# A new beginning for a per-image mixed 3x3 convolution block: image 0 in halves, weights convolution by convolution, a ring of four buffers

## The chip, the cores and the metric

The kernel runs on one core of one Trainium2 chip. The metric is the device time of one execution in microseconds; the number compared is the median of several runs. One further execution is recorded by the profiler.

## What is computed

Sixteen images of 32 channels and 96 x 96 pixels in float32. Each is normalised channel by channel, and for each image a softmax gate over seven experts mixes its own two sets of 3x3 kernels:

```python
x_n     = (x - mean) / sqrt(var + 1e-5)                 # per image and channel
gate    = softmax(mean(x_n) @ gate_w.T + gate_b)         # 7 values per image
kw1,kb1 = sum_e gate[e] * experts_1[e] + conv1           # kernels and bias of this image
kw2,kb2 = sum_e gate[e] * experts_2[e] + conv2
out     = x + x_n + conv3x3(relu(conv3x3(x_n, kw1) + kb1), kw2) + kb2
```

## The kernel before

Channels and row groups share the 128 partitions (32 channels x 4 rows), so an image is a tile `img` of 128 x 24 x 96, in a ring of six. Both convolutions work on float16 pairs: a value is a high part (HI) and a low part (LO), and three products (HI x HI, HI x LO of the weights, LO x HI) are added in PSUM. A convolution is five groups (`pg0` to `pg4`) of 18 matmuls: per product and kernel column one with the straight weights and tile (`a`) and one with the crossed ones (`c`), whose partition halves are exchanged. The two of a pair run side by side in the array.

The steps of an image are these. `load` (SP queue). `statistics` and `aggregate` (VectorE), `gather_rows` (TensorE, `pstat`), `channel_moments` (VectorE), `coefficients` (GpSimd), which give mean and scale and the gate's input `gwp`. `logits` (TensorE), `softmax_in`, `exponentials` (ScalarE), `softmax_out`. `mixture`, seven VectorE steps over `bank` (all kernels of both convolutions, 386 wide) into `mix`; `weights_high` casts the high part on ScalarE, `weights` subtracts the low part on VectorE. The crossed copy comes by DMA (`cross_weights`), for the first two images (EARLY) by two VectorE copies (`cross_early`). The input: `normalise` writes float32 `xh` and `high_part` the HI half of `a1` on ScalarE, `low_part` the LO half on GpSimd in four pieces, `cross1` sends both to `c1` by DMA. Then conv1; `hidden` (ScalarE, twice per group: `hid` float32 and HI of `a2`), `hidden_low` (VectorE), `clear_rim`, `cross2` (two ScalarE copies), conv2; `residual` (GpSimd), `finish` (VectorE), `store`.

Each engine has its list of instructions written out by hand: a beginning, and then `slot(s)` once per image. In slot s TensorE does conv1 of image s and conv2 of image s-1, with `gather_rows` of image s+2 between groups 3 and 4 of conv1. TensorE's beginning ends with four of the five conv1 groups of image 1 and slot 1 opens with `gather_rows` of image 3, then group 4 of image 1. Lists are in order: an instruction waits for semaphores, and all behind it on its engine waits too.

The raw kernels (`natural`) arrive on ScalarE's DMA queue, are spread (`pad_kernels`), turned by TensorE (`transpose_kernels(n)`, n = 0 to 3 for conv1, 4 to 7 for conv2) and copied into `bank` by ScalarE (even n) and VectorE (odd n).

## Time and profile before

| | |
|---|---|
| median of 3 runs | 365.44 us (365.11 to 365.81) |
| profiled execution, device time | 366.37 us |
| its span, first to last instruction | 364.6 us |
| busy: TensorE matmul / VectorE / ScalarE / GpSimd | 87% / 79% / 69% / 53% |
| chain that ended last: TensorE / VectorE / DMA | 60% / 19% / 10% |
| mean granted TensorE clock | 0.98 |

The device time is 1.8 us longer than the span in the profiled execution. A share of busy time is a mean over a beginning, a long regular stretch and an end; the stretches differ, and so they are read apart.

### The profile page before, as it was taken

How to read it: one execution, taken by the hardware profiler on the slowest of the kernel's cores; microseconds unless marked ns; L12 is line 12 of the kernel's file. 1: busy time of each engine (PE TensorE's matmuls, PEld its weight loads, DVE VectorE, ACT ScalarE, POOL GpSimd, SP SyncE). 2: the span in 40 equal slices, each digit the busy share in tenths (PEclk: the TensorE clock that was granted, in tenths of full speed). 3: DMA queues.
4: the chain of work that ended last, by engine and by line, in shares of the span. 5: the costliest groups of instructions: out<-in, count | busy, mean ns of one | idle time of the engine just before them, and what ended most of it. 6: DMA issues, size and time to landing. Idle time of an engine off the chain costs nothing.

```text
span 364.6 us, 7708 instructions
## 1 busy us (share of the span) xinstructions
PE 317.4 (87%) x2983; PEld 200.6 (55%) x2983; DVE 288.0 (79%) x651; ACT 252.8 (69%) x278; POOL 192.9 (53%) x236
## 2 busy tenths in 40 slices
PE   2327664499999999999899989999999999999994
PEld 2216432257565656565566646575756565676552
DVE  4699945698989989898979896989989898693432
ACT  1155219896878778787869695878887797965710
POOL 8039517492838475665739391848475656921000
PEclk9999989599999999999999999999999999999999
DMA  9932930599989797989997899979898977575055
GB/s 197 222 70 57 227 77 3 120 167 202 210 186 211 177 216 179 211 174 205 191 217 145 201 199 220 173 180 219 186 211 188 211 173 151 122 174 142 0 131 130
DMA packets 109379, 60.86 MB, mean 167 GB/s; under 512 B 102944, under 2 KB 105248, under 8 KB 109344
## 3 DMA queue, kind: packets, MB, share of 16 engines
q1 hardware_dynamic: 108544, 59.79, 78.9%
q10 hardware_dynamic: 608, 0.59, 0.6%
q8 instruction: 23, 0.38, 0.5%
q14 instruction: 12, 0.10, 0.1%
q0 software_dynamic: 192, 0.01, 0.0%
HBM read 19.47 MB, written 18.87 MB: 105 GB/s over the span
## 4 chain that ended last, share of the span: by engine, by line
PE 60%; DVE 19%; DMA 10%; SPq 3%; ACT 3%; POOL 2%; issue 2%; ACTq 0%; DVEq 0%; POOLq 0%
PE pg L376 56%; DVE mix L646 9%; DMA wts<-wts 7%; DVE a L677 3%; DVE wts L663 3%; DMA c<-a 2%; PE pg L339 2%; DVE stats L601 2%; PE pstat L359 2%; POOL a L865 1%; SPq L260 1%; DMA natural<-in_L_conv_conv_w 1%; SPq L296 1%; SPq L287 1%; ACT xh L491 1%
## 5 line engine op out<-in xcount | busy, mean ns | idle before, releaser
L376 PE MATMUL pg<-a,wts 128*64 128x480 f16 (+1 forms) x1440 | 292.2, 362 | 11.3 <-DMA c<-a 6.3
L376 PE MATMUL pg<-c,wts 128*64 128x480 f16 (+1 forms) x1440 | 297.7, 366 | 0.0
L376 PEld LDWEIGHTS pg<-c,wts 128*64 128x64 f16 x1440 | 154.5, 110 | 72.2 <-issue 1.1
L376 PEld LDWEIGHTS pg<-a,wts 128*64 128x64 f16 x1440 | 154.8, 110 | 43.3 <-issue 8.7
L865 POOL TENSOR_TENSOR a<-xh,a 128x576 f16<-128x576 f32 x64 | 79.1, 1268 | 13.4 <-POOL col L873 9.3
L534 ACT ACTIVATE hid<-pg,col 128x480 f32<-128x480 f32 x80 | 52.5, 657 | 46.7 <-PE pg L376 37.1
L646 DVE SCALAR_TENSOR_TENSOR mix<-bank,gate,mix 128x386 f32<-128x386 f32 x96 | 73.9, 770 | 2.4
L846 POOL TENSOR_TENSOR col<-col,minus_half 128x1 f32<-128x1 f32 x16 | 13.5, 841 | 111.6 <-DVE col L619 111.6
L550 ACT COPY c<-a 64x2352 f32<-64x2352 f32 x32 | 68.9, 2152 | 2.1 <-DVE a L677 1.9
L677 DVE TENSOR_TENSOR a<-hid,a 128x480 f16<-128x480 f32 x80 | 52.5, 657 | 21.2 <-ACT a L534 20.9
L693 DVE SCALAR_TENSOR_TENSOR img<-pg,img 128x480 f32<-128x480 f32 (+1 forms) x80 | 48.2, 632 | 13.6 <-PE pg L376 13.1
L879 POOL TENSOR_SCALAR img<-img,col 128x1152 f32<-128x1152 f32 x32 | 57.9, 1817 | 0.1
L534 ACT ACTIVATE a<-pg,col 128x480 f16<-128x480 f32 x80 | 52.5, 656 | 0.0
L601 DVE BATCH_NORM_STATS2 stats<-img 128x6 f32<-128x384 f32 x96 | 45.6, 544 | 0.1
L491 ACT ACTIVATE xh<-img,col 128x2304 f32<-128x2304 f32 x16 | 36.9, 2306 | 11.3 <-POOL col L847 11.3
L496 ACT ACTIVATE a<-img,col 128x2304 f16<-128x2304 f32 (+1 forms) x17 | 37.3, 2194 | 6.5 <-POOL col L847 6.5
L663 DVE TENSOR_TENSOR wts<-mix,wts 128x384 f16<-128x384 f32 x16 | 20.6, 1288 | 0.3 <-ACT wts L519 0.3
L359 PE MATMUL pstat<-triples,same 128*128 128x12 f32 x32 | 7.0, 293 | 15.4 <-DVE triples L608 15.4
L519 ACT CAST wts<-mix 128x384 f16<-128x384 f32 x16 | 8.2, 512 | 15.9 <-DVE mix L646 15.9
L359 PEld LDWEIGHTS pstat<-triples,same 128*128 128x128 f32 x32 | 5.5, 215 | 21.4 <-DVE triples L608 16.0
L616 DVE COPY col<-pstat 128x1 f32<-128x1 f32 x16 | 2.5, 157 | 18.6 <-PE pstat L359 18.6
L339 PE MATMUL pg<-ident,padded 128*128 128x128 f32 x24 | 5.6, 424 | 8.4 <-DVE padded L707 8.4
(61 smaller groups left out, 143.4 us busy)
## 6 DMA issues: line engine op xcount, KB each, us to landing
c<-a SPq DMA_DIRECT2D x28, 588.0 KB, 7.0
img<-in_x SPq DMA_DIRECT2D x56, 288.0 KB, 7.0
out<-img SPq DMA_DIRECT2D x60, 180.0 KB, 3.0
out<-img SPq DMA_DIRECT2D x60, 108.0 KB, 2.6
wts<-wts SPq DMA_DIRECT2D x28, 96.0 KB, 2.5
c<-a SPq DMA_DIRECT2D x8, 294.0 KB, 5.9
img<-in_x SPq DMA_DIRECT2D x16, 144.0 KB, 5.0
out<-img SPq DMA_DIRECT2D x4, 120.0 KB, 2.1
```

The costliest lines, as they stand in the source:

```text
L376: last = nc.tensor.matmul(pg[g][side * 64:side * 64 + 64, at:at + nb * W].rearrange("p (b w) -> p b w", w=W), wts[s.c % WSETS][kind][:, v, ...
L491: nc.scalar.activation(xh[t.parity][:, :, :], img[t.ring][:, :, :], ACT.Identity, bias=c[:, NBIAS:NBIAS + 1], scale=c[:, RSTD:RSTD + 1]).t ...
L496: return nc.scalar.activation(a1[t.parity][:, HI, b0:b1, 1:1 + W], img[t.ring][:, b0:b1, :], ACT.Identity, bias=c[:, NBIAS:NBIAS + 1], sca ...
L534: last = nc.scalar.activation(o, pg[g][:, 0:SPG * W].rearrange("p (b w) -> p b w", w=W), ACT.Relu, bias=c[:, B1:B1 + 1], scale=HS / WS)
L550: last = nc.scalar.copy(d, a[:, :, first:first + NB * RP // 2])
L601: last = nc.vector.bn_stats(stats[t.ring][:, j, :], flat[:, j * SC:(j + 1) * SC])
L646: nc.vector.scalar_tensor_tensor(out=mix[:, (e + 1) % 2, :, :], in0=bank[:, e, :, :], scalar=gate[t.ring][:, e:e + 1], in1=bank[:, E, :, : ...
L663: nc.vector.tensor_tensor(st[:, :, LO, :], mix[:, E % 2, :, 0:TAPS], st[:, :, HI, :], ALU.subtract).then_inc(w_ok, 1)
L677: nc.vector.tensor_tensor(a2[s.parity][:, LO, j0:j1, 1:1 + W], hid[g_parity(s, g)][:, :, :], a2[s.parity][:, HI, j0:j1, 1:1 + W], ALU.subt ...
L693: nc.vector.scalar_tensor_tensor(out=r, in0=pg[g][:, 0:(b1 - b0) * W].rearrange("p (b w) -> p b w", w=W), scalar=1.0 / (WS * HS), in1=r, o ...
L865: last = nc.gpsimd.tensor_tensor(a1[t.parity][:, LO, b0:b1, 1:1 + W], xh[t.parity][:, b0:b1, :], a1[t.parity][:, HI, b0:b1, 1:1 + W], ALU. ...
L879: last = nc.gpsimd.tensor_scalar(img[t.ring][:, b0:b1, :], img[t.ring][:, b0:b1, :], c[:, RS1:RS1 + 1], c[:, RB:RB + 1], ALU.mult, ALU.add)
```

## The change

SP: only image 0 is loaded in halves (`x_half`); image 1 comes whole. The high and low parts of images 0 and 1 are crossed in halves of the rows, HI of image 0 ahead of the load of image 2, LO behind it. ScalarE: the six loads of `natural` wait for the first half of image 0. Images 0 and 1 get their weights for one convolution at a time: `mixture_early` runs seven steps 193 wide, `weights_early` subtracts and copies for one convolution; conv1's come first and release `w_early`, conv2's come later and release `w_crossed`. `low_part` of an early image waits for `w_early`. TensorE runs conv1 of images 0 and 1 in two passes, all groups with HI, then all with LO, and all five groups of image 1 are done ahead of slot 1; transposes 6 and 7 stand within image 0's conv1. `hid` becomes a ring of four, two of them in `natural`, which is free by then, and `hidden` waits for the `hidden_low` of four groups earlier instead of two. The slots keep their order, and slot 0 of ScalarE and GpSimd is written out in the beginning.

```diff
+        spare = natural[:, :, :, :].rearrange("p a b c -> p (a b c)")
+        hid = [h[:, :, :] for h in hid] + [spare[:, i * SPG * W:(i + 1) * SPG * W].rearrange("p (j w) -> p j w", w=W)
+                                           for i in range(2)]
...
             load(Sample(0, 0))
             load(Sample(0, 1))
+            cross1_early(Sample(0, 0), HI, 0)
+            cross1_early(Sample(0, 0), HI, 1)
             load(Sample(0, 2))
-            cross1(Sample(0, 0))
+            cross1_early(Sample(0, 0), LO, 0)
+            cross1_early(Sample(0, 0), LO, 1)
+            cross1_early(Sample(0, 1), HI, 0)
+            cross1_early(Sample(0, 1), HI, 1)
             load(Sample(0, 3))
-            cross1(Sample(0, 1))
+            cross1_early(Sample(0, 1), LO, 0)
+            cross1_early(Sample(0, 1), LO, 1)
...
+            early_conv1(first, 0, HI)
+            early_conv1(first, 1, HI)
+            transpose_kernels(6)
+            transpose_kernels(7)
+            early_conv1(first, 2, HI)
+            gather_rows(second)
...
+            gather_rows(third)
+            for g in range(GRP):
+                early_conv1(second, g, HI)
+            early_conv1(second, 0, LO)
+            early_conv1(second, 1, LO)
+            logits(third)
...
-                run(conv1_group, s, 0, 1, 4)
+                run(conv1_group, s, 0, 2, 4)
...
             def load_kernels():
+                act.wait_ge(x_half, LOAD)
...
-                if not (s.known(0) and g < 2):
-                    act.wait_ge(lo2_ok, s.number * GRP + g - 1)
+                if s.number * GRP + g >= len(hid):
+                    act.wait_ge(lo2_ok, s.number * GRP + g + 1 - len(hid))
...
+            def mixture_early(t, v, e0, e1):
...
+                for e in range(e0, e1):
+                    if e > 0:
+                        dve.wait_ge(mix_step, (weight_sets(t, v) - 1) * (E - 1) + e)
+                    nc.vector.scalar_tensor_tensor(
+                        out=mix[:, (e + 1) % 2, v, :], in0=bank[:, e, v, :], scalar=gate[t.ring][:, e:e + 1],
+                        in1=bank[:, E, v, :] if e == 0 else mix[:, e % 2, v, :],
+                        op0=ALU.mult, op1=ALU.add).then_inc(mix_step if e < E - 1 else mix_ok, 1)
...
+            def weights_early(t, v):
+
+                dve.wait_ge(whi_ok, weight_sets(t, v))
+                st, cr = wts[t.c % WSETS][STRAIGHT], wts[t.c % WSETS][CROSSED]
+                link(nc.vector.tensor_tensor(st[:, v, LO, :], mix[:, E % 2, v, 0:TAPS], st[:, v, HI, :], ALU.subtract))
+                for a, b in ((0, 1), (1, 0)):
+                    last = nc.vector.tensor_copy(halves(cr)[a][:, v].rearrange("p a b -> p (a b)"),
+                                                 halves(st)[b][:, v].rearrange("p a b -> p (a b)"))
+                if v == 0:
+                    last.then_inc(w_early, 1)
+                else:
+                    last.then_inc(w_crossed[t.ring], 32)
...
             coefficients(Sample(0, 0))
+            low_part(Sample(0, 0))
             coefficients(Sample(0, 1))
-            low_part(Sample(0, 0), 0, PARTS)
-            low_part(Sample(0, 1), 0, PARTS)
+            low_part(Sample(0, 1))
+            coefficients(Sample(0, 2))
+            residual_bias(Sample(0, 0))
+            residual(Sample(0, 0))
```

Three places show how the lists move. On VectorE the first is its start, after the constants; before, it read (a row is line, operation, output and inputs with their numbers):

```order
L707 COPY padded<-natural 128x3x96 x2
L735 TENSOR_SCALAR bank<-pg1 128x4x96
L735 TENSOR_SCALAR bank<-pg3 128x4x96
L707 COPY padded<-natural 128x3x96 x2
L735 TENSOR_SCALAR bank<-pg1 128x4x96
L735 TENSOR_SCALAR bank<-pg3 128x4x96
L601 BN_STATS stats0<-img0 128x6 x6
L606 BN_AGGR mv0<-stats0 128x2
```

The same place of VectorE's list now:

```order
L677 BN_STATS stats0<-img0 128x6 x6
L692 BN_AGGR mv0<-stats0 128x2
L693 TENSOR_SCALAR triples0<-row,mv0 128x4
L694 TENSOR_SCALAR triples0<-row,mv0 128x4
L820 COPY padded<-natural 128x3x96 x2
L702 COPY col0<-pstat 128x1
L703 BN_AGGR col0<-pstat 128x2
L704 TENSOR_SCALAR col0<-col0 128x1
L705 TENSOR_SCALAR col0<-col0 128x1
```

The statistics of image 0 have moved ahead of the kernels, and the moments of image 0 stand behind the first spreading of the kernels.

The second place is VectorE ahead of the statistics of image 3. Before:

```order
L677 TENSOR_TENSOR a2_0<-hid0,a2_0 128x5x96
L684 MEMSET a2_0 32x2x96
L601 BN_STATS stats3<-img3 128x6 x6
L625 SCALAR_TENSOR_TENSOR logit2<-pgate,gbias 128x7
L628 TENSOR_REDUCE col2<-logit2 128x1
L677 TENSOR_TENSOR a2_1<-hid1,a2_1 128x5x96
L606 BN_AGGR mv3<-stats3 128x2
```

Now, from the end of image 0's `hidden_low` steps:

```order
L743 SCALAR_TENSOR_TENSOR mix<-bank,gate0,mix 128x193 x6
L770 TENSOR_SCALAR col0<-mix 128x1
L711 SCALAR_TENSOR_TENSOR logit2<-pgate,gbias 128x7
L714 TENSOR_REDUCE col2<-logit2 128x1
L755 TENSOR_TENSOR wts0_0<-mix,wts0_0 128x192
L757 COPY wts0_1<-wts0_0 64x384 x2
L743 SCALAR_TENSOR_TENSOR mix<-bank,gate1 128x193
L743 SCALAR_TENSOR_TENSOR mix<-bank,gate1,mix 128x193 x6
L770 TENSOR_SCALAR col1<-mix 128x1
L755 TENSOR_TENSOR wts1_0<-mix,wts1_0 128x192
L757 COPY wts1_1<-wts1_0 64x384 x2
L677 BN_STATS stats3<-img3 128x6 x6
```

The conv2 weights of images 0 and 1 now stand between the last `hidden_low` of image 0 and the statistics of image 3.

The third place is ScalarE behind group 4 of image 0's `hidden`. Before:

```order
L534 ACTIVATE a2_0<-pg4,col0 128x5x96
L496 ACTIVATE a1_0<-img2,col2 128x24x96
L550 COPY c2_0<-a2_0 64x2352 x2
L510 ACTIVATE expo2,col2<-logit2,col2 128x7
L534 ACTIVATE hid1<-pg0,col1 128x480
```

And now:

```order
L600 ACTIVATE a2_0<-pg4,col0 128x5x96
L577 CAST wts0_0<-mix 128x192
L616 COPY c2_0<-a2_0 64x2352 x2
L541 ACTIVATE xh0<-img2,col2 128x2304
L554 ACTIVATE a1_0<-img2,col2 128x24x96
L577 CAST wts1_0<-mix 128x192
L571 ACTIVATE expo2,col2<-logit2,col2 128x7
L600 ACTIVATE hid1<-pg0,col1 128x480
```

The two casts of conv2 weights stand ahead of and behind `cross2` of image 0 and the input of image 2.

## Rows read from the trace of the kernel before

**Rows 1.** Chain of waits, regular stretch: start us, us, what ran.

```profile
98.28 3.09 DMA wts<-wts
101.41 7.53 PE pg L376 x71
...
214.68 4.65 DMA wts<-wts
```

**Rows 2.** Busy time by stretch: PE, PEld, DVE, ACT, POOL, then clock, DMA, GB/s.

```profile
60.00:69.00 9.00, 0.58 (x4) 0.55 (x6) 5.06 (x16) 8.96 (x11) 4.83 (x4) 0.66 0.16 31
...
90.00:108.95 18.95, 18.70 (x183) 11.52 (x181) 17.24 (x39) 15.27 (x17) 11.75 (x13) 1.00 0.97 199
```

**Rows 3.** Timeline, TensorE: start us, us, line, operation, count, [idle before <-releaser].

```profile
6.94 2.79 PE L339 MATMUL pg<-ident,padded 128*128 128x128 f32 x12 [6.94 <-DVE padded L707]
...
33.15 0.35 PE L376 MATMUL pg<-a,wts 128*64 128x384 f16 x1 [0.60 <-DVE wts L670]
...
48.99 0.32 PE L376 MATMUL pg<-a,wts 128*64 128x384 f16 x1 [5.13 <-DMA c<-a]
...
68.42 0.60 PE L359 MATMUL pstat<-triples,same 128*128 128x12 f32 x2 [9.51 <-DVE triples L608]
...
82.13 0.36 PE L376 MATMUL pg<-c,wts 128*64 128x480 f16 x1
```

**Rows 4.** Start: timeline of two rows, and DMA issues with us to landing.

```profile
1.68 0.48 ACTq L474 DMA_DIRECT2D natural<-in_L_conv_conv_w  x1
...
5.88 0.92 DVE L707 COPY padded<-natural 128x288 f32<-128x288 f32 x2 [2.42 <-DMA natural<-in_L_conv_conv_w]
...
natural<-in_L_conv_conv_w ACTq DMA_DIRECT2D x1, 36.0 KB, 4.1
...
img<-in_x SPq DMA_DIRECT2D x2, 144.0 KB, 3.7
```

**Rows 5.** Timeline of VectorE and GpSimd, 14 to 74 us.

```profile
14.63 2.86 DVE L601 BATCH_NORM_STATS2 stats<-img 128x6 f32<-128x384 f32 x6
...
22.56 0.17 DVE L625 SCALAR_TENSOR_TENSOR logit<-pgate,gbias 128x7 f32<-128x7 f32 x1
...
23.64 0.23 DVE L636 TENSOR_SCALAR gate<-expo,col 128x7 f32<-128x7 f32 x1
...
25.54 3.24 DVE L646 SCALAR_TENSOR_TENSOR mix<-bank,gate,mix 128x386 f32<-128x386 f32 x5
...
28.80 5.40 POOL L865 TENSOR_TENSOR a<-xh,a 128x576 f16<-128x576 f32 x4
...
30.49 2.60 DVE L670 COPY wts<-wts 64x768 f16<-64x768 f16 x2
...
34.92 7.45 DVE L646 SCALAR_TENSOR_TENSOR mix<-bank,gate,mix 128x386 f32<-128x386 f32 x6
...
43.54 0.72 DVE L670 COPY wts<-wts 64x768 f16<-64x768 f16 x2
...
70.88 0.88 POOL L846 TENSOR_TENSOR col<-col,minus_half 128x1 f32<-128x1 f32 x1 [4.58 <-DVE col L619]
...
73.34 0.47 POOL L856 TENSOR_TENSOR gwp<-table,col 128x7 f32<-128x7 f32 x1
```

**Rows 6.** Timeline of ScalarE and VectorE, 42 to 77 us, and one DMA issue.

```profile
42.82 0.65 ACT L534 ACTIVATE hid<-pg,col 128x480 f32<-128x480 f32 x1
...
43.92 0.66 ACT L534 ACTIVATE hid<-pg,col 128x480 f32<-128x480 f32 x1
...
59.02 2.32 ACT L496 ACTIVATE a<-img,col 128x2304 f16<-128x2304 f32 x1
61.23 4.31 ACT L550 COPY c<-a 64x2352 f32<-64x2352 f32 x2
...
76.52 1.45 DVE L663 TENSOR_TENSOR wts<-mix,wts 128x384 f16<-128x384 f32 x1
...
wts<-wts SPq DMA_DIRECT2D x2, 96.0 KB, 2.2
```

More of the change, by code:

```diff
@@ L49 @@
 EARLY = 2
-WARM = 7
+WARM = 8
 PARTS = 4
@@ L371, in products @@
                 for image, weight in pairs:
-                    if early(s) and v == 0 and g == 0 and image == LO:
-                        wait_low_part(s)
                     for kw in range(3):
@@ L744, in _ @@
             row_constants()
+            statistics_first(0)
+            statistics_first(1)
+            aggregate(first)
             pad_kernels(0)
+            channel_moments(first)
+            repeat_table()
             copy_kernels(1)
+            copy_table()
             copy_kernels(3)
             pad_kernels(1)
+            softmax_in(first)
+            softmax_out(first)
+            mixture_early(first, 0, 0, E)
+            weights_early(first, 0)
             copy_kernels(5)
+            statistics(second)
@@ new lines, in _ @@
+            weights_early(second, 0)
+            channel_moments(third)
+            hidden_low(first, 0)
+            clear_rim(first, 0)
+            hidden_low(first, 1)
+            hidden_low(first, 2)
+            hidden_low(first, 3)
+            hidden_low(first, 4)
+            clear_rim(first, GRP - 1)
+            mixture_early(first, 1, 0, E)
+            softmax_in(third)
+            weights_early(first, 1)
+            mixture_early(second, 1, 0, E)
+            weights_early(second, 1)
```

339 lines of the change are left out of this document (190 added, 149 removed).

## Prediction, written before the changed kernel was run

> **What bounds the kernel now.** I read the chain of waits first, then the busy time by stretch, then the timelines of the beginning. In the regular stretch the chain of one image runs from `gather_rows` through moments, mixture and weights on VectorE to the DMA that crosses the weights, which lands after 3.09 us, and then through four conv1 groups of 7.53 us [rows 1] to the next `gather_rows`. TensorE is busy 18.70 of 18.95 us there [rows 2], so the loop and TensorE are about equally long. Nothing in the slots changes, so what the change is worth is how much sooner the regular stretch is entered. I measure it where conv1 of image 2 begins, at 82.13 us [rows 3].
>
> The beginning before is no TensorE stage. The first conv1 matmul starts at 33.15, behind the crossed weights of image 0; TensorE then waits 5.13 us up to 48.99 for crossed rows, and 9.51 us up to 68.42 for the statistics of image 3 [rows 3]. In that last wait ScalarE is busy 8.96 of 9 us [rows 2]: VectorE cannot finish image 3's `aggregate` before ScalarE has delivered `hidden` of image 1. So a gain at 33 reaches 68 only if it also gets through the lists of ScalarE and VectorE. I follow four stages, each ending at an event all later work needs. All times are my sums unless a row is named.
>
> **Stage A, up to the first conv1 weights.** The kernels' DMAs now wait for half of image 0. Its fourth transfer is issued at about 2.2; transfers of this size issued first landed in 3.7 us [rows 4]. With no kernels beside it I take 6.0 (ends 5.6 and 7.8). Three issues of about 0.48 follow; the last began at 1.68 in the kernel before and landed after 4.1 us, VectorE starting on it at 5.88 [rows 4]. So the kernels are there at 6.0 + 1.0 + 4.1 = 11.1, say 11.2. The statistics of image 0 (2.86 [rows 5]) lie in the wait. Spreading costs 0.92 [rows 4], 12.1; transposing 2.8 [rows 3], 15.0; turning and copying the table 0.8, 15.8. VectorE then copies and spreads for 1.5 more, 17.3, over which `gwp` and `logits` are hidden. Softmax took 1.3 from 22.56 to the end of the gate [rows 5]: 18.6. Seven mixture steps 193 wide: the trace has none. Of 386 one takes 3.24 / 5 = 0.65; a step of 7 elements takes 0.17 to 0.2 [rows 5]. Bounds are half (0.32) and the whole (0.65); fixed part 0.2 plus half of 0.45 gives 0.43, which I take. 7 x 0.43 = 3.0, 21.6. The cast 0.4 (bounded by a `hidden` step, 1.10 / 2 = 0.55 [rows 6]), the subtraction 0.4, two copies at most the 0.72 of double width [rows 5], 0.5: **22.9**. Before it was 33.15, so 10.2 sooner. GpSimd waits for `w_early`, so nothing slows these copies. The crossed HI halves leave at 16.4 and 19.6 and are hidden. Eight warming matmuls end at about 22.3.
>
> **Stage B, up to image 1's conv1 weights.** VectorE: copy 0.6, statistics of image 1 2.9, aggregate 0.7, 27.1. TensorE: twelve pairs (0.2 each), six transposes, six pairs, `gather_rows`, 28.6. Moments 0.5, 29.1. GpSimd from the first coefficient to `gwp` takes 2.9 (70.88 to 73.81 [rows 5]), 32.0; TensorE reaches `logits` of image 1 at 32.3, after 24 pairs: 32.9. VectorE's statistics of image 2 end at 33.2, its load having moved behind image 0's HI crossing; softmax and exponentials, 34.1 on ScalarE. There `hidden` 0 and 1 (1.1 each [rows 6]) and two halves of `normalise` (1.2 each) stand ahead of the cast: 38.7, and VectorE's mixture, done at 37.7, hides behind them. Cast, subtraction and copies: **40.0**. TensorE has waited some 4.5 us by then. Around the wait of 9.51 the granted clock is 0.66 [rows 2, 3]; whether the clock falls here is open, the price is 1.7 us, and it lies on TensorE, which is not late here.
>
> **Stage C, up to the end of image 0's conv2 mixture.** Moments 0.5; five `hidden_low` and two rims 3.3: 43.8. Then seven steps of 0.43, the first two still beside image 1's `low_part` (5.40 for its four pieces, so to 45.4); beside it six full steps took 7.45, or 1.24 each [rows 5]. I take 4.1: **47.9**.
>
> **Stage D, up to `gather_rows` of image 3.** This is the place that gives back most of the gain. ScalarE: cast 0.4, `cross2` 4.3 (4.31), `normalise` 2.2 and `high_part` 2.2 (59.02 to 61.23) [rows 6], and only then the cast of image 1's conv2 weights: 57.4. VectorE has finished their mixture at about 55 and waits for that cast, and the statistics of image 3 are queued behind it. The three steps of `weights_early` then run beside `low_part` of image 2, which starts on the same ScalarE step. Copies of double width took 1.30 each beside such pieces and 0.36 without [rows 5]; ends for the three steps are 0.9 and 3.9, and I take 3.5, since a copy beside GpSimd lasted as long as one of its pieces (5.40 / 4 = 1.35), whatever its own work. 60.9. Statistics 2.9, `hidden_low` 0.6, aggregate 0.7: **65.1**, against 68.42. TensorE has waited since about 51.5.
>
> The Trainium skill (SBUF — State Buffer, SBUF: two separate sides) says that VectorE steps with two SBUF inputs or in a two-port mode and a GpSimd step hold a shared port pair exclusively, the later one blocking for the whole instruction. By it, halving the width buys nothing beside GpSimd, so it speaks against this split; the 1.30 beside 1.35 agrees. With widths scaled instead (0.65 a copy) the sum would be 1.5 us lower.
>
> **Stage E.** From aggregate to the end of `weights` took 68.4 to 77.97 (76.52 + 1.45 [rows 6]), 9.6, in an order that stays: 74.7. Two issues 0.6 and a landing of 2.2 [rows 6]: conv1 of image 2 starts at **77.5**. TensorE's other work in between (conv2 of image 0, nine us and 1.7 for the low clock) ends at about 76, since group 4 of image 1 is gone from there. Before: 82.13. Difference **4.6 us**.
>
> **The ring of four** is costed at nothing: ScalarE's waits for VectorE stand in the beginning alone, and C and D go through other waits. Without it ScalarE's `hidden` 2 to 4 would follow VectorE's steps, a bit over 1 us at C. The profiled execution lies 0.9 above the median (366.37 and 365.44). 366.4 - 4.6 = 361.8 for a profiled one; **360.8** for the median.
>
> **Rivals.**
> (1) The whole 10.2 us is carried through: 355.2. It needs VectorE and ScalarE to be early at stage D; against it stand the 9.1 us of ScalarE work between the two casts. 7%.
> (2) The kernels queue behind image 1's load instead of sharing with it. The load is 1.18 MB, at 0.2 MB per us [rows 2] nearly 6 us; they would be there at about 14: 363.6. Against it: beside image 0's load they landed in 4.1. The Trainium skill (DMA: Bandwidth & Descriptors, Queues, rings and completion order) says that each DMA engine takes turns between its queues by packets, which agrees with that 4.1 and would keep 360.8. 12%.
> (3) Full-width price for half-width steps (0.65): 1.5 at A, 1.5 at C, together 363.8. 10%.
> (4) Slower than before: the weights' DMA in the regular stretch meets other traffic. It is in the chain of seven images; it landed after 3.09 in one and 4.65 in another [rows 1]. The loads and stores follow the new phase. If all seven slip by 1.5, 10.5 is added: 371.3. It decides from 4.6 / 7 = 0.66 us an image. For it: the spread exists; against: every slot restarts from the same `gather_rows`, so the phases repeat. 7%.
> (5) Stage D takes up everything (nothing gained, 365.4): `gather_rows` of image 3 would have to come at 69.7, most of (2) and (3) at once. 5%.
>
> **How the numbers follow.** The forecast case with its own spread holds 59%. The terms' bounds: kernels at 10.1 or 12.7 (with a late half image), steps of 0.32 (1.5 less over A and C), weights at D 0.9 (2.6 less) or 3.9. That is 356 to 363; not all fall together, so 357.3 below, and 364.2 above to take in (2) and (3). A measurement can tell about 0.2% (0.7 us) from no change. Faster than 364.7: (1), (2), nearly all of (3) and the forecast, 0.87; within: 0.05; slower: 0.08.
>
> **What would show it.** First conv1 matmul at about 23; `w_early` of image 1 at 40; a TensorE wait of 10 to 14 us ahead of `gather_rows` of image 3, released by VectorE's `triples`; copies of `weights_early` over 1 us beside GpSimd; a short wait on the crossed weights ahead of conv1 of image 2; intervals between later `gather_rows` as before, near 19.3. The forecast is wrong if image 3's `gather_rows` falls outside 62 to 67, or if the regular stretch changes its period.

## The result: 0.6% slower

Measured again beside each other, the kernel before took 367.56 us (median of 20, 365.11 to 370.25) and the changed one 369.38 (median of 20, 367.18 to 373.1): a ratio of 1.006, 95% interval 1.0037 to 1.0082 (by the two medians alone it is 1.005). The forecast was 360.8 with a range from 357.3 to 364.2, so it was wrong, and on the wrong side. The profiled execution of the changed kernel took 369.45 us; its span was 367.6, against 364.6.

First the chain of waits of the changed kernel (start us, us, what), in the beginning and around the first interval of the regular stretch.

```profile
2.18 3.09 DMA img<-in_x
...
6.21 7.79 DMA natural<-in_L_conv_conv_w
...
14.02 0.90 DVE padded L820 x2
...
79.55 0.52 SPq L320
...
80.11 2.18 DMA wts<-wts
...
89.87 0.34 PE pstat L392 x2
...
97.95 1.04 SPq L320
...
99.04 3.79 DMA wts<-wts
...
102.88 7.53 PE pg L407 x71
110.41 0.32 PE pstat L392 x2
```

Then the timeline of TensorE (start, us, line, tiles, [idle before <-releaser]), to be held against [rows 3].

```profile
25.45 0.35 PE L407 MATMUL pg<-a,wts 128*64 128x384 f16 x1 [1.34 <-DVE wts L757]
...
41.84 0.53 PE L407 MATMUL pg<-a,wts 128*64 128x384 f16 x1 [4.53 <-DVE wts L757]
...
69.97 0.60 PE L392 MATMUL pstat<-triples,same 128*128 128x12 f32 x2 [15.71 <-DVE triples L694]
```

The first conv1 matmul starts at 25.45 instead of 33.15, 7.7 us sooner. Then TensorE waits 15.71 us instead of 9.51, and `gather_rows` of image 3 comes at 69.97, 1.55 later than before (68.42). Conv1 of image 2, my mark for the entry, begins at 82.33 against 82.13. So all of the early gain is gone at the entry. From there to the end some 2.8 us more are lost. I read the slots by the aggregate step that opens `channel_moments` on VectorE, in these two kernels about half a microsecond behind each `gather_rows`: from image 4's to the last one's, eleven intervals, it takes 213.4 us before (90.07 to 303.47) and 216.2 after (90.30 to 306.54). The first of them is 19.31 before and 20.54 after.

Where the time between 42 and 69 went is in VectorE's timeline of the changed kernel.

```profile
42.26 1.36 DVE L790 TENSOR_TENSOR a<-hid,a 128x480 f16<-128x480 f32 x1
...
43.97 1.27 DVE L790 TENSOR_TENSOR a<-hid,a 128x480 f16<-128x480 f32 x1
45.16 3.32 DVE L790 TENSOR_TENSOR a<-natural,a 128x480 f16<-128x480 f32 x2
48.39 0.65 DVE L790 TENSOR_TENSOR a<-hid,a 128x480 f16<-128x480 f32 x1
...
49.85 2.70 DVE L743 SCALAR_TENSOR_TENSOR mix<-bank,gate,mix 128x193 f32<-128x193 f32 x6
...
61.95 1.31 DVE L755 TENSOR_TENSOR wts<-mix,wts 128x192 f16<-128x192 f32 x1 [2.94 <-ACT wts L577]
63.30 2.40 DVE L757 COPY wts<-wts 64x384 f16<-64x384 f16 x2
65.73 2.86 DVE L677 BATCH_NORM_STATS2 stats<-img 128x6 f32<-128x384 f32 x6
```

And GpSimd beside it:

```profile
41.86 6.09 POOL L978 TENSOR_TENSOR a<-xh,a 128x576 f16<-128x576 f32 x4 [8.56 <-DVE wts L757]
```

Three things stand here. The `hidden_low` steps of image 0 (0.65 alone) take 1.3 to 1.7 us each as long as `low_part` of image 1 runs, whose four pieces take 1.5 each. The mixture behind them runs at full pace (0.45 a step). And VectorE waits 2.94 us for ScalarE's cast of image 1's conv2 weights, after which three short steps take 3.75 us with the statistics of image 3 behind them, as forecast.

### The profile page after: what moved, and what is told of

Same layout as the page of the kernel before. It is cut to its first block, busy times and chain, and to the rows that moved or that the text cites. A ratio compares the mean times of both kernels' runs of the same rounds, so it can differ in the third digit from the quotient of the medians.

```text
span 367.6 us, 7743 instructions
## 1 busy us (share of the span) xinstructions
PE 317.1 (86%) x2985; PEld 200.4 (55%) x2985; DVE 294.7 (80%) x671; ACT 253.4 (69%) x283; POOL 190.8 (52%) x236
## 3 DMA queue, kind: packets, MB, share of 16 engines
q1 hardware_dynamic: 109120, 59.79, 77.5%
## 4 chain that ended last, share of the span: by engine, by line
PE 58%; DVE 24%; DMA 10%; ACT 3%; issue 2%; SPq 1%; ACTq 0%; DVEq 0%
PE pg L407 55%; DVE mix L729 9%; DMA wts<-wts 7%; DVE a L790 4%; DVE wts L784 3%; DMA natural<-in_L_conv_conv_w 2%; DVE mix L743 2%; DVE stats L677 1%; PE pstat L392 1%; ACT c L616 1%; ACT xh L541 1%; SPq L320 1%; DVE wts L757 1%; DMA img<-in_x 1%; PE pg L372 1%
## 5 line engine op out<-in xcount | busy, mean ns | idle before, releaser
L729 DVE SCALAR_TENSOR_TENSOR mix<-bank,gate,mix 128x386 f32<-128x386 f32 x84 | 63.0, 750 | 2.0
L541 ACT ACTIVATE xh<-img,col 128x2304 f32<-128x2304 f32 (+1 forms) x18 | 37.7, 2094 | 17.9 <-POOL col L956 17.9
L600 ACT ACTIVATE natural<-pg,col 128x480 f32<-128x480 f32 x40 | 26.3, 657 | 21.1 <-PE pg L407 21.1
L600 ACT ACTIVATE hid<-pg,col 128x480 f32<-128x480 f32 x40 | 26.2, 656 | 18.4 <-PE pg L407 17.7
L790 DVE TENSOR_TENSOR a<-natural,a 128x480 f16<-128x480 f32 x40 | 28.4, 712 | 11.1 <-ACT a L600 11.0
L790 DVE TENSOR_TENSOR a<-hid,a 128x480 f16<-128x480 f32 x40 | 27.5, 687 | 5.7 <-ACT a L600 5.5
L784 DVE TENSOR_TENSOR wts<-mix,wts 128x384 f16<-128x384 f32 x14 | 19.4, 1386 | 0.0
L987 POOL TENSOR_TENSOR col<-col 128x1 f32<-128x1 f32 x16 | 7.1, 443 | 12.0 <-DVE col L778 6.3
```

What stands on the lines that cost most here:

```text
L541: return nc.scalar.activation(xh[t.parity][:, b0:b1, :], img[t.ring][:, b0:b1, :], ACT.Identity, bias=c[:, NBIAS:NBIAS + 1], scale=c[:, RS ...
L600: last = nc.scalar.activation(o, pg[g][:, 0:SPG * W].rearrange("p (b w) -> p b w", w=W), ACT.Relu, bias=c[:, B1:B1 + 1], scale=HS / WS)
L729: nc.vector.scalar_tensor_tensor(out=mix[:, (e + 1) % 2, :, :], in0=bank[:, e, :, :], scalar=gate[t.ring][:, e:e + 1], in1=bank[:, E, :, : ...
L784: nc.vector.tensor_tensor(st[:, :, LO, :], mix[:, E % 2, :, 0:TAPS], st[:, :, HI, :], ALU.subtract).then_inc(w_ok, 1)
L790: nc.vector.tensor_tensor(a2[s.parity][:, LO, j0:j1, 1:1 + W], hid_of(s, g), a2[s.parity][:, HI, j0:j1, 1:1 + W], ALU.subtract).then_inc(l ...
```

## Experiments

Eighteen kernels ran. Each ratio is against the kernel before, run in the same job (its medians were 367.3 to 367.9); the times of events are from one profiled execution of each kernel. The names are explained in the sections below; the table has what they use: `gather_rows` of image 3; the aggregate of image 4's `channel_moments`, called the entry; the eleven intervals behind it; all in us from the profiled execution.

| kernel | gather 3 | entry | eleven intervals | ratio, 95% interval |
|---|---|---|---|---|
| before | 68.42 | 90.07 | 213.4 | 1 |
| changed | 69.97 | 90.30 | 216.2 | 1.006 (1.0037 to 1.0082) |
| a_late1 | 66.20 | 86.54 | 216.1 | 0.994 (0.992 to 0.996) |
| a_low | 66.63 | 88.10 | 214.5 | 0.996 (0.994 to 0.999) |
| a_cast | 66.94 | 88.68 | 214.4 | 1.002 (0.999 to 1.004) |
| a_stats | 69.29 | 90.43 | 214.1 | 0.999 (0.996 to 1.002) |
| b_ring | 66.46 | 88.48 | 215.9 | 0.998 (0.996 to 1.001) |
| a_two | 65.03 | 88.76 | 213.7 | 0.995 (0.992 to 0.998) |
| a_three | 64.58 | 86.39 | 214.3 | 0.991 (0.988 to 0.995) |
| a_best | 58.92 | 89.67 | 214.4 | 0.997 (0.994 to 1.001) |
| a_best_split | 58.34 | 85.29 | 214.7 | 0.989 (0.983 to 0.995) |
| a_three_split | 63.53 | 84.10 | 214.9 | 0.985 (0.979 to 0.990) |
| a_all | 63.75 | 84.50 | 210.8 | 0.976 (0.969 to 0.982) |
| after_all | 70.63 | 91.25 | 211.2 | 0.994 (0.991 to 0.997) |
| before_all | 68.62 | 90.66 | 210.0 | 0.989 (0.986 to 0.993) |
| a_all2 | 63.45 | 85.58 | 223.3 | 1.010 (1.005 to 1.016) |

### The kernels behind image 1's load (a_late1)

```diff
             load(Sample(0, 0))
+            sp.wait_ge(w_in[0], 16 * 3)
             load(Sample(0, 1))
```

> The changed kernel, with one wait more: SP issues the load of image 1 only when the kernels of conv1 have landed. Theory Q (the kernels' transfers share the DMA engines with image 1's load and are slowed by it): they land at 10 to 10.5 us instead of 14.0, since 4.1 us was their landing beside one image in the kernel before, and image 1, needed at 25.9, still comes in time. Rival (they are slow for a reason of their own, their small rows): still 13 us or later. Theory L (the lists of the beginning carry every microsecond on to the regular stretch): gather_rows of image 3 moves from 69.97 to about 66.3 and the ratio to the kernel before goes from 1.006 to 0.996. Rival R (the regular stretch gives it back through the landing of the crossed weights): gather_rows of image 3 moves, the total stays within 0.3% of 1.006.

Chain of waits of a_late1, the same place as above:

```profile
4.21 3.87 DMA img<-in_x
8.10 1.49 DVE stats L678 x3
...
10.33 0.81 DVE padded L821 x2
```

The kernels are used at 10.33, straight behind the statistics, instead of 14.02; the chain goes through image 0's own load. The first conv1 matmul starts at 21.68, `gather_rows` of image 3 at 66.20, both 3.8 us sooner, and the median falls to 365.56. At the entry all of it is still there (86.54 for 90.30). Rival (2) of the prediction was right in what it named: beside image 1's 1.18 MB, whose issue ran from 4.74 to 11.05, the last of the kernels' three transfers (144, 108 and 36 KB on one queue) landed 7.79 us after its issue, and with image 1 held back 2.6 us after it. Whether they waited behind those bytes or shared the engines with them, these runs do not tell apart.

### GpSimd beside hidden_low (a_low)

```diff
             low_part(Sample(0, 0))
             coefficients(Sample(0, 1))
-            low_part(Sample(0, 1))
             coefficients(Sample(0, 2))
+            pool.wait_ge(mix_ok, 3)
+            low_part(Sample(0, 1))
```

(`softmax_in(third)` moves behind the mixture of image 1 to fit.)

> The changed kernel with low_part of image 1 on GpSimd held back until the conv2 mixture of image 0 is done; coefficients of image 2 stand ahead of it, and softmax_in of image 2 moves on VectorE behind the conv2 mixture of image 1. Theory P (a VectorE step with two inputs takes as long as a GpSimd piece when both run): the five hidden_low of image 0 take 0.6 us each instead of 1.3 to 1.7, the mixture ends at about 48.5 instead of 52.55, gather_rows of image 3 comes at about 66 instead of 69.97, ratio 0.995. Rival (hidden_low was slow for another reason, the buffers in the old place of the kernels or waiting on ScalarE): the steps stay over 1.2 us and gather_rows stays at 69 to 70. Rival 2: the contention only moves, onto the mixture of image 1, and ScalarE's cast waits for it: gather_rows over 68.

VectorE of a_low, timeline:

```profile
42.43 0.65 DVE L790 TENSOR_TENSOR a<-hid,a 128x480 f16<-128x480 f32 x1
...
43.43 0.66 DVE L790 TENSOR_TENSOR a<-hid,a 128x480 f16<-128x480 f32 x1
44.00 1.22 DVE L790 TENSOR_TENSOR a<-natural,a 128x480 f16<-128x480 f32 x2
...
49.72 1.12 DVE L755 TENSOR_TENSOR wts<-mix,wts 128x192 f16<-128x192 f32 x1 [0.23 <-ACT wts L577]
50.87 2.40 DVE L757 COPY wts<-wts 64x384 f16<-64x384 f16 x2
```

The first of these steps starts within 0.2 us of the one in the changed kernel, and all five take 0.61 to 0.66. The mixture's end moves from 52.55 to 49.3: 3.25 us. The contention itself moved on: `low_part` now starts at 49.38, the subtraction and copies of `weights_early` take 3.5 us instead of 1.9, and `gather_rows` of image 3 comes at 66.63, 3.3 us sooner: the whole gain is still there. At the entry 2.2 are. The steps lengthen to much the same 1.1 to 1.7 us whatever their own width, which agrees with the exclusive port pair that the Trainium skill describes (SBUF — State Buffer, SBUF: two separate sides).

### The order on ScalarE (a_cast) and on VectorE (a_stats)

```diff
             normalise(third)
-            high_part(third)
             weights_high_early(second, 1)
+            high_part(third)
```

> The changed kernel with one ScalarE step moved: the cast of image 1's conv2 weights stands ahead of high_part of image 2 instead of behind it. Theory L: VectorE gets the cast at 59.5 instead of 61.9, and its three steps of weights_early take 0.9 us instead of 3.75, because low_part of image 2 on GpSimd has not begun; statistics and aggregate of image 3 then end at about 64.9, bounded by hidden of image 1 on ScalarE (63.5), and gather_rows of image 3 comes at 65.0 instead of 69.97; conv1 of image 2 at 77.4 instead of 82.33; ratio 0.993. Rival R: the same times in the beginning, but the total within 0.3% of 1.006.

VectorE of a_cast:

```profile
59.30 0.36 DVE L755 TENSOR_TENSOR wts<-mix,wts 128x192 f16<-128x192 f32 x1 [0.74 <-ACT wts L577]
59.69 0.52 DVE L757 COPY wts<-wts 64x384 f16<-64x384 f16 x2
60.24 2.86 DVE L677 BATCH_NORM_STATS2 stats<-img 128x6 f32<-128x384 f32 x6
63.14 1.43 DVE L790 TENSOR_TENSOR a<-hid,a 128x480 f16<-128x480 f32 x1
```

The wait falls from 2.94 to 0.74 and the three steps from 3.75 to 0.91, since `low_part` of image 2 has not started. `gather_rows` of image 3 comes 3.0 us sooner, at 66.94, of which 0.45 was there already at `gather_rows` of image 1, ahead of the edit. It falls 1.9 us short of the 65.0 expected, because the steps behind the statistics now run beside `low_part` (`hidden_low` 1.43, the two `triples` steps 0.87 and 1.28, against 0.66, 0.23 and 0.22 in a_low). At the entry 1.6 are left, and the ratio is 0.4% lower (1.002, not the 0.993 expected), which is as much; the intervals of the two ratios touch.

```diff
+            statistics(Sample(0, 3))
             mixture_early(second, 1, 0, E)
             weights_early(second, 1)
-            statistics(Sample(0, 3))
```

> The changed kernel with the statistics of image 3 moved on VectorE ahead of the conv2 mixture of image 1, into the time in which VectorE waits for ScalarE's cast. Theory L: the mixture then ends at about 61.8, just before the cast, the three steps of weights_early stay at 3.75 us beside GpSimd, and gather_rows of image 3 comes at 67.1 instead of 69.97 (2.9 us); ratio 0.998. Rival R: total within 0.3% of 1.006.

In a_stats the profiled execution was 1.3 us behind at `gather_rows` of image 1 (31.82 for 30.52), where the granted clock was low (below), so I compare from there: to that of image 3 it took 37.5 us against 39.5. The ratio is 0.999, 0.7% below the changed kernel's. In the profile none of that stands at the entry (90.43 for 90.30); the eleven intervals are 2.1 us shorter.

### The ring of four alone (b_ring)

```diff
-            return (s.c * GRP + g) % 2
+            return (s.number * GRP + g) % 4
```

> The kernel before with the ring of four buffers for the conv1 groups alone (two in the place of the raw kernels, and the wait four groups back). Costed at nothing in the regular stretch. In the beginning ScalarE waited 3.4 and 4.9 us for VectorE's hidden_low of image 0; with four buffers these waits go, but ScalarE then waits for the next conv1 groups, which TensorE starts at 48.99. Expected: gather_rows of image 3 up to 1 us sooner than 68.42, ratio 0.997 to 1.000. Rival: the two buffers in the old place of the kernels make the slots slower, ratio over 1.003.

ScalarE no longer waits 3.43 and 4.87 us for VectorE in the beginning, and `gather_rows` of image 3 comes 2.0 us sooner than before. Of these it had 0.9 already at the first `gather_rows` (17.38 for 18.30), so the ring gave 1.1, what the prediction put on it in passing. At the median the ratio is 0.998, with an interval that holds 1. Its eleven intervals took 2.5 us longer than before; 1.7 of that is one interval in which TensorE waited for a crossing (5.04 us to land), the granted clock fell to a mean of 0.82, and the four groups took 9.21 us instead of 7.53. The changed kernel with the old ring of two was not run, so what the ring does there is not shown.

### Two and three together (a_two, a_three, a_best)

a_two joins a_late1 and a_cast; a_three adds a_low.

> The changed kernel with the late load of image 1 and the early cast together. They act on different stages of one chain, so the gains should add: 3.8 us (late load, measured) and 3.0 us (early cast, measured) give gather_rows of image 3 at 63.2 and conv1 of image 2 at about 76.5; ratio 0.987 to 0.990. Rival R (the regular stretch gives a part back, since it is entered with the crossed weights as the last to come): not under 0.992.

> The late load, the early cast and the held-back low_part of image 1 together: gather_rows of image 3 at about 59.5, ratio 0.978 to 0.982 if all of it is carried on. Rival: with VectorE and ScalarE this early TensorE's own work or the crossings of image 1 end last in the beginning, gather_rows at 62 or more, ratio over 0.985.

a_two missed its range (0.995 for 0.987 to 0.990), and so did a_three, which ran in 364.03 us (0.991 for 0.978 to 0.982). Part of it is that the granted clock was low around 22 to 25 us in both (below). Yet a_three's `gather_rows` of image 3 is 5.4 us sooner than the changed kernel's and its entry only 3.9. a_best added more warming matmuls and the statistics and aggregate of image 3 ahead of the mixture of image 1 (so that its `gather_rows` of image 3 leaves the path: 58.92).

> The changed kernel with five edits: late load of image 1, early cast of image 1's conv2 weights, low_part of image 1 held back until the conv2 mixture of image 0, 15 warming matmuls, and on VectorE the statistics of image 3 behind that mixture (beside low_part, where statistics were not slowed) with its aggregate ahead of hidden_low of image 1 instead of behind. Theory L: VectorE ends the aggregate at about 57.5, TensorE's conv1 of image 1 ends at about 59.6 and is then the last to come; gather_rows of image 3 at 59.7, the second one after it at 99.2 instead of 110.4; ratio 0.972 to 0.980. Rival: the crossed low parts of image 1 or the weights of image 2 (behind hidden of image 1 on VectorE) end last; the second gather_rows at 102 or later, ratio over 0.984.

It missed the slower end of its range by 7 us, and its chain of waits shows where:

```profile
72.73 1.26 SPq L320
...
74.03 5.01 DMA wts<-wts
...
79.09 10.14 PE pg L408 x71
89.23 0.32 PE pstat L393 x2
```

SP's timeline of a_best just ahead:

```profile
65.47 7.15 SPq L277 DMA_DIRECT2D img<-in_x  x4
72.73 1.90 SPq L320 DMA_DIRECT2D wts<-wts  x2
```

The weights of image 2 are ready and their crossing is issued at 72.73, 0.1 us behind the last transfer of image 4's load. It lands at 79.04. The same pair of rows in the other kernels:

| kernel | issue of image 4's load ends | crossing issued | landed | behind the load's end | TensorE waits |
|---|---|---|---|---|---|
| changed | 75.28 | 79.55 | 82.29 | 7.0 | 0.44 |
| a_late1 | 71.57 | 75.78 | 78.52 | 7.0 | none to speak of |
| a_low | 74.70 | 76.21 | 80.08 | 5.4 | 1.46 |
| a_cast | 75.31 | 76.52 | 80.67 | 5.4 | 1.23 |
| a_two | 73.43 | 74.61 | 79.07 | 5.6 | 2.22 |
| a_three | 72.99 | 74.16 | 78.38 | 5.4 | 1.93 |
| a_best | 72.62 | 72.73 | 79.04 | 6.4 | 4.84 |

At this place no crossing landed sooner than 5.4 us behind the load's last issue, however early it was issued. That is what took early gains back, and it depends on where they were won. The load stands on SP behind the crossed rows of image 2, which wait for GpSimd. In a_late1 everything is sooner, the load with the rest, and the gain of 3.8 us reaches the entry whole. In a_cast, a_low and a_best the weights gain more than the load does; the crossing moves closer to the load, and it lands where the load lets it. The Trainium skill has the rule for one queue (DMA: Bandwidth & Descriptors, Two DMAs through the same engine are not ordered): descriptors of one queue start in order. The table agrees, though it would look the same if the two transfers only shared the DMA engines. In a_best the clock adds to the price: TensorE stood still for 4.84 us, the granted clock fell from 1.00 to 0.50 (the lower level, 1.2 GHz), and the four groups of conv1 took 10.14 us instead of 7.53.

### The load's last transfer behind the crossing (a_best_split, a_three_split, a_split5)

If that reading holds, the cure is on SP: three of the four transfers ahead of the crossing and one behind. For image 4 alone:

```diff
+FIRST = lambda n: 3 if n == 4 else 4
...
-                for g in range(G):
+                for g in range(0, FIRST(t.number)):
...
                 run(cross_weights, s, 0, 2)
+                run(load_rest, s, 2, 4)
```

> The combined kernel (five edits), in which the last of image 4's four load transfers is now issued behind the crossing of image 2's weights instead of ahead of it. In the combined kernel that crossing was issued 0.1 us behind the load (72.73 behind 72.62), took 1.26 us to issue and landed 5.01 us later, at 79.05; TensorE waited 4.84 us for it, the granted clock was 0.50 from 78 to 84, and gather_rows of image 4 came 10.1 us later, at 89.23. Theory queue: the crossing lands where the transfers queued ahead of it end (7.0, 5.4, 5.6, 5.4 and 5.4 us behind the end of the load's issue in five kernels); with three transfers ahead, whose issue ends about 1.8 us sooner, it lands at 76.3, TensorE waits about 2.1 us, the clock does not fall, and gather_rows of image 4 comes 7.5 to 8 us later, at 84 to 84.5; the time falls by 3 to 5 us against the combined kernel's ratio of 0.997, to a ratio of 0.984 to 0.990. Theory statistics: the last transfer now lands near 79.5 and VectorE's statistics of image 4 (77.72) follow it; hidden_low of image 2 and the later mixtures follow that, and gather_rows of image 4 or the weights of image 3 come no sooner: ratio 0.994 to 1.000. Theory noise: the early gain was never there, and a second profile of nearly the same kernel scatters about it.

> The same edit (last transfer of image 4's load behind the crossing of image 2's weights) on the version with three edits, ratio 0.991 before. There the crossing was issued 1.2 us behind the load and landed after 3.65 us, at 78.4, with a TensorE wait of 1.93. Theory queue: it lands 1.4 to 1.8 us sooner, near 76.8, where TensorE has just ended its own earlier work (76.5), so gather_rows of image 4 comes 1.5 to 1.9 sooner, at 84.2, and the ratio is 0.986 to 0.988. Theory statistics: image 4's statistics (78.06, no wait) now wait 1.5 us for the load, and what is won at the crossing is lost by the weights of image 3: ratio 0.990 to 0.993.

a_best's entry moved from 89.67 to 85.29 and its ratio from 0.997 to 0.989. The crossing still took 3.91 us to land (77.28, 5.9 behind the third transfer's issue), a microsecond more than expected, but the clock stayed up. Of the 4.4 us, 0.6 was there already at `gather_rows` of image 3. a_three's entry moved from 86.39 to 84.10, but there 1.05 of the 2.3 us had come in the beginning, since this profiled execution was free of the low clock that a_three's had; the edit's own share is 1.2 us. TensorE's wait for the crossing is

```profile
76.12 0.35 PE L416 MATMUL pg<-a,wts 128*64 128x384 f16 x1 [0.46 <-DMA wts<-wts]
```

0.46 instead of 1.93; ratio 0.985. Both went the way of the theory of the queue, though the intervals of the ratios with and without the edit still overlap in both pairs.

For the first regular interval of the changed kernel I first tried a delay of the start, six idle matmuls behind `gather_rows` of image 3:

```diff
                 run(gather_rows, s, 2, 3)
+                if s.number == 1:
+                    for _ in range(6):
+                        nc.tensor.matmul(pset[:, P:2 * P], ident[:, :], same[:, :], start=True, stop=True)
```

> The changed kernel with six idle matmuls (like those of warm_up) between gather_rows of image 3 and conv2 of image 0, so that conv1 of image 2 starts at about 83.8 instead of 82.33 and TensorE, not the crossed weights, comes last there. Theory R (the phase at the entry decides how image 3's weights land): the crossed weights of image 3 land after about 3.0 us, the first interval between gather_rows is 19.3 instead of 20.5, and the total does not rise, ratio 1.002 to 1.006. Rival (the longer regular stretch of the changed kernel is chance from run to run): everything comes 1.5 us later, ratio 1.010, and the first interval is as before the pad.

That told nothing: the delay moved the load and the crossing alike (1.7 us between them, with it and without), the interval stayed at 20.45, and the ratio was 1.0087 (1.0056 to 1.0117). The test that moves one against the other is a_split5, the split for image 5 (`n == 5`) in the changed kernel.

> The changed kernel, with the last transfer of image 5's load behind the crossing of image 3's weights. It asks why the first regular interval (gather_rows of image 4 to that of the next image) is 20.54 us in the changed kernel and 19.32 before: over ten kernels that interval is 20.5 to 20.8 where that crossing is issued 1.5 to 1.8 us behind the load, and 18.9 to 19.6 where it is issued 2.6 or more behind it. Theory queue: the gap decides; now three transfers stand ahead, the gap is 3.4, the crossing lands near 101 instead of 102.8, and the interval is 18.9 to 19.4, the second gather_rows of the regular stretch at about 109 instead of 110.41, ratio about 0.3 % below that of the changed kernel (1.006), near 1.002. Theory statistics: statistics of image 5, which wait 0.37 us for this load already, start about 1.5 us later and the interval stays at 20.5 for that reason. Theory coincidence: the interval stays at 20.5 though the crossing lands sooner.

Its chain of waits:

```profile
90.24 0.34 PE pstat L400 x2
...
98.33 0.52 SPq L327
98.89 3.12 DMA wts<-wts
...
109.59 0.34 PE pstat L400 x2
```

The interval is 19.35, as before the change (19.32), instead of 20.54; the crossing is issued in 0.52 us and lands after 3.12, not 1.04 and 3.79. All eleven intervals take 213.7 us, against 216.2 and, before the change, 213.4. The ratio is 1.001 (0.998 to 1.004), whose interval just meets the changed kernel's. The longer first interval was the crossing close behind the load.

### Everywhere (a_all, after_all, before_all, a_all2)

```diff
+FIRST = lambda n: 4 if n < 4 else 3
```

> The version with three edits, with the last load transfer of each image from 4 on issued behind the crossing of the weights. In it six of eleven intervals ended on that crossing, which landed after 2.9 to 4.8 us, and were 19.1 to 21.0 long instead of the 18.9 that TensorE needs: 6.6 us in all. Theory queue: the load ahead makes the crossing late in every slot; it lands after 2.2 to 3 us everywhere, and 3 to 5 us go: ratio 0.977 to 0.984. Theory stores: what meets the crossing in the later slots is not the load of the same slot but the stores and crossed images; then the landing stays spread from 2.9 to 4.8 us and the ratio is 0.989 to 0.994. Slower than 0.994 if statistics, which follow the load, become the last to come.

a_all is a_three with this: 358.82 us, ratio 0.976 (0.969 to 0.982), the fastest kernel here and faster than both. Its eleven intervals take 210.8 us. Its chain of waits now runs through the moved transfer:

```profile
110.82 0.52 SPq L327
...
112.03 3.68 DMA img<-in_x
115.73 1.64 DVE stats L686 x4
```

> The changed kernel, with nothing else but the last load transfer of each image from 4 on issued behind the crossing of the weights. The changed kernel enters the regular stretch at gather_rows of image 4 at 89.87, the kernel before at 89.63, but its eleven intervals up to the last gather_rows take 216.2 us against 213.4, and with three edits and this one 211.1. Theory queue: what the change lost (0.6 %) it lost to crossings queued behind loads; with the load's last transfer moved, the eleven intervals take 211 to 212 us, the time is 364 to 365 and the ratio 0.988 to 0.993, and it is the same, within 0.3 %, as the kernel before with this one edit. Theory entry: the loss comes from what else the new beginning does to the phase of the slots; then it stays 0.4 to 0.8 % behind the kernel before with the same edit.

> The kernel before, with nothing else but the last load transfer of each image from 4 on issued behind the crossing of the weights. Its crossings are issued about 3.2 us behind the loads already and land after 2.9 to 4.65 us. Theory queue: the eleven intervals fall from 213.4 to 211 to 212, ratio 0.992 to 0.996, and the change is then worth nothing (within 0.3 %) beside it. Theory stores: at this phase the load is out of the way already and the crossings meet other transfers; ratio 0.998 to 1.002.

The edit alone is worth more than the whole change: 0.989 on the kernel before, where I expected 0.992 to 0.996, and from 1.006 to 0.994 on the changed one, just above what I expected. The eleven intervals fell to 210.0 and 211.2. The two versions stand 0.4% apart, with intervals that overlap; whether the change is worth nothing or slightly less than nothing with the queue gone stays open.

> The version with four edits (ratio 0.9755), with the last two load transfers of each image behind the crossing of the weights instead of the last one. Theory statistics: in the version with one transfer behind it VectorE's statistics already wait 0.9 to 1.0 us for that transfer in each slot; a second one lands about 1.5 us later, VectorE follows it, and with little idle time left there each interval grows by 0.3 to 1 us: ratio 0.985 to 1.005. Theory queue alone: the crossing has still less ahead of it (it landed after 1.7 to 4.2 us), intervals reach the 18.9 us of TensorE, ratio 0.970 to 0.975.

With two transfers behind the crossing, VectorE's statistics wait for them in every slot:

```profile
99.60 2.86 DVE L686 BATCH_NORM_STATS2 stats<-img 128x6 f32<-128x384 f32 x6 [2.40 <-DMA img<-in_x]
```

Every interval is 20.15 to 20.74 long and the ratio 1.010. So of none, one and two transfers one is the right share: the load is on the path on both sides, ahead of the weights' crossing and ahead of the statistics.

### The clock in the beginning (a_warm), and the kernels' wait for image 0 (a_nowait)

In a_stats, a_two, a_three, a_pad, a_nowait and after_all the granted clock fell to between 0.50 and 0.83 somewhere between 20 and 30 us, in a_pad up to 32. Common to them is a warm-up of sixteen matmul records that ran fast and ended early, with a wait of 3.0 us behind it; a_three:

```profile
17.04 1.95 PE L383 MATMUL pg<-same,ident 128*128 128x128 f32 x16
22.00 0.53 PE L408 MATMUL pg<-a,wts 128*64 128x384 f16 x1 [3.02 <-DVE wts L758]
```

In the profiled execution of the changed kernel the warm-up took 3.00 us and the wait was 1.34. a_warm raises the warming matmuls:

```diff
-WARM = 8
+WARM = 15
```

> The changed kernel with 15 warming matmuls instead of 8. Theory C (TensorE waits for the first weights behind the warming matmuls, the granted clock falls in some executions at 24 to 28 us, and the first passes of conv1, which stand ahead of gather_rows of image 1, then run at 1.2 GHz): no fall of the clock there, gather_rows of image 1 never after 31 us, and the median 0.5 to 1.5 us lower, ratio 1.002 to 1.005. Rival (the clock there costs nothing in the end, or the longer warming itself delays conv1): ratio 1.006 or more.

The warm-up took 3.51 us, TensorE waited 1.45, and the clock stayed at 1.00 up to 40 us; `gather_rows` of image 1 came at 30.39. The time did not move: 1.007 (1.004 to 1.010), beside 1.006. From the first conv1 matmul to `gather_rows` of image 1 it takes 6.0 to 6.3 us with the low clock and 5.1 without (6.03 in a_three, 5.08 in a_late1), so the low clock costs about 1 us, and 2.5 in a_pad. But the changed kernel's own profiled execution was free of it too; how many of its other executions have it, no run shows, and for this kernel the longer warm-up is worth nothing that can be measured.

```diff
-                act.wait_ge(x_half, LOAD)
```

> The changed kernel without the wait for half of image 0 ahead of the kernels' loads (as in the kernel before). The kernels then land at about 6 us, and the halves of image 0 later, at 7.8 and 10.6, as traced before. VectorE's spreading of the kernels stands behind the statistics of image 0, which end at about 12.1: it starts at 12.9 instead of 14.0. Theory Q/L: 1.1 us sooner all along, gather_rows of image 3 at about 68.9, ratio 1.003. Rival (loading image 0 first is what makes the new beginning quick): spreading no sooner than 14, ratio 1.006 or more.

Without the wait for image 0's first half, the kernels' transfers run beside the loads from the start, and now image 0 is late: its halves are used at 8.13 and 11.25 instead of landing at 5.29 and 7.87. First conv1 matmul at 24.82, ratio 1.002 (0.999 to 1.004): the same bytes in another order. What helps is that image 1 waits (a_late1), not that the kernels wait for image 0.

## Why the prediction was wrong

The mechanisms named were mostly there; two terms in front of the entry were too small, and the stretch behind it was taken for constant. In the profiled executions this adds up: forecast 361.8, conv1 of image 2 at 82.33 instead of 77.5 (4.8), the eleven intervals 2.8 longer, together 369.4, and 369.45 was measured. At the median 0.9 more is missing. The forecast started from 365.44, the median of three executions; twenty gave 367.56. From that start it would have been 363.0, still 6.4 too low.

- **Stage A, the failed term.** "So the kernels are there at 6.0 + 1.0 + 4.1 = 11.1, say 11.2." The first half of image 0 landed early (5.29 for 6.0), but the kernels at 14.0: the landing term was 7.79 us, not 4.1. I had priced it by a row in which they ran beside image 0's load alone [rows 4], and put the queue behind image 1 down as a rival of 12%. It cost 2.8 us there, and a_late1, in which the landing is 2.6, wins 3.8 at the first matmul. The rest of A held: a mixture step took 0.45 (I took 0.43), the first matmul came at 25.45 (22.9 forecast). The rule of the Trainium skill that I leant on (DMA: Bandwidth & Descriptors, Queues, rings and completion order: each engine takes turns between queues) let me expect that the kernels would pass; here it did not keep the landing short, 7.79 us against 4.10. In both kernels the 36 KB that land last stand behind 252 KB of their own queue; what differs is the load beside them.
- **Stage B held.** 41.84 for 40.0: 0.7 us of A's delay were made up.
- **Stage C, the second failed term.** The end of image 0's conv2 mixture came at 52.55, not 47.9; 1.8 us of that came from A and B, 2.8 is C's own. I priced the five `hidden_low` steps at 0.6, as if nothing ran beside them, and two mixture steps as slowed; it was the other way round. Four of them cost 1.3 to 1.7 us instead of 0.65. The row from which to know it was there [rows 5]: full mixture steps at 1.24 beside `low_part`. a_low shows the cause: with `low_part` held back the same steps took 0.61 to 0.66 and the mixture ended 3.25 us sooner.
- **Stage D held as to its kind and size**: from the mixture's end to `gather_rows` of image 3, 17.4 us measured, 17.2 summed; the three steps of `weights_early` 3.75 (3.5). It started 4.6 us too late, and so rival (5), nothing gained, is what happened up to the entry (its mark was 69.7, measured 69.97). I had given it 5% and asked for (2) and (3) together. (2) came, (3) did not (a step took 0.45), and the slowed `hidden_low` stood in its place: the mark was met by another road than the one I had named.
- **Stage E held**: 12.36 us from `gather_rows` to conv1 of image 2 (12.4). The landing of 2.2 had a condition that I did not state: it holds where the crossing is issued 2.7 us or more behind the load (a_split5, a_late1, changed); 1.2 to 1.5 us behind it, it was 3.3 to 3.9 (a_low, a_cast, a_two, a_three). a_three reached the forecast's `gather_rows` of image 3 (64.58 for 65.1), and its ratio was 0.991 where the forecast's is 0.987. Which of the two the forecast case would have met, no run shows.
- **The ring** held as far as b_ring shows: 1.1 us in the beginning, nothing measurable at the median.
- **The regular stretch.** "Every slot restarts from the same `gather_rows`, so the phases repeat" is the sentence that made rival (4) a 7% case. The phases differ: SP's last issue of image 5's load came 1.7 us ahead of the crossing, before the change 3.1. The first interval was 1.2 longer, and later ones together 1.6. a_split5 shows the cause of the first. The later 1.6 is nearly gone there too (0.3 left in all), but in one profiled execution, and I can't tell it from the scatter between kernels (213.4 to 217.3 over the kernels without the split everywhere).

My check was right in form: I had written that `gather_rows` of image 3 outside 62 to 67 or another period would refute the forecast, and both came.

## What to carry to other kernels

In this kernel a transfer's landing time went by what had been issued ahead of it, on its own queue and on others, more than by its size (96 KB took from 2.2 to 5.0 us): price it by when the bytes ahead have drained, and look at where each earlier step will move the issue to. If a small transfer is urgent and a large one is not, issue the large one in pieces around it, and look on both sides, since the large one has a reader too (one piece of four behind gave 1.1 to 1.6%, the second cost 3.5%). A gain in a beginning is worth only what arrives at the first step that everything later waits for; put a number on each queue between the two.

## What the hardware showed that I had not expected

- At the entry a crossing of 96 KB never landed sooner than 5.4 us behind the last issue of a load of 1.18 MB ahead of it on the same queue, and took 5.01 us when issued 0.1 behind it, 2.2 when 4.3 behind. In later slots, where stores and crossed rows run as well, it was 4.9 (b_ring) to 7.2 us behind that issue.
- A load of 36 KB, behind 252 KB of its own and on another engine's queue than the image's, landed after 7.79 us beside 1.18 MB, after 4.1 beside image 0's load alone, and after 2.6 with no image load being issued beside it (a_late1).
- A warm-up that ends early can be worse than one that ends late: sixteen records in 1.95 us left 3.0 us of idle time and the clock fell to 0.50; in 3.00 us they left 1.3 and it stayed at 1.00.
- In the regular stretch of the changed kernel long intervals (19.9 to 21.2) alternate, up to the ninth, with ones of 18.88 in which TensorE does not wait: a slot that starts late behind a crossing is followed by one whose crossing is in time.
